# One more wait ahead of each scatter in the expert phase of an attention and mixture-of-experts kernel

## What is computed

```python
x = x + cross_attention(ctx_768, layernorm(x), mask)        # 64 batches of 128 tokens, width 256
h = layernorm(x)                                            # 8192 tokens
topk_idx, topk_w = route(h)                                 # 4 of 32 experts for each token
gate_vals = silu(h @ gate_w[e].T); up_vals = h @ up_w[e].T  # 128 wide
expert_out = (gate_vals * up_vals) @ down_w[e].T            # 256 wide
mixed = (expert_out of the 4 chosen * topk_w).sum(1)
x = x + mixed + shared_expert(h)
```

## Time and profile before

| | us |
|---|---|
| median of 3 runs | 1436.4 (1429.46 to 1436.93) |
| the profiled execution, own time | 1446.1 |
| its span, first to last instruction | 1444.1 |
| mean granted TensorE clock, share of 2.4 GHz | 0.984 |
| PE / ACT / DVE / POOL busy, share of the span | 93% / 72% / 67% / 42% |

### The profile page before, as it was taken

The page is one execution under the profiler, slowest core; times in us unless marked ns, Lnnn a source line. Parts: engine busy times, 40 slices in busy tenths (PEclk is TensorE's granted clock), DMA queues, the critical chain, the costliest instruction groups (busy, mean ns, idle before and its releaser), DMA issues.

```text
span 1444.1 us, 33057 instructions
## 1 busy us (share of the span) xinstructions
PE 1341.7 (93%) x8730; PEld 1042.9 (72%) x8730; DVE 963.0 (67%) x4500; ACT 1042.4 (72%) x2861; POOL 610.4 (42%) x662
## 2 busy tenths in 40 slices
PE   7999999999999999999798989988888889989997
PEld 4666666666666676666587878878788878878886
DVE  5578888888888888887863444444444444447888
ACT  5999999999999999998515555555555655553432
POOL 1004544544444554454553555555555555550000
PEclk8999999999999999999899999999999999999998
DMA  7145455445445544544865444444444444419886
GB/s 263 71 144 179 144 182 189 148 146 181 163 137 177 181 139 155 181 150 163 317 206 188 142 144 146 145 143 138 146 143 144 145 137 142 119 31 339 302 296 228
DMA packets 145780, 246.78 MB, mean 171 GB/s; under 512 B 22075, under 2 KB 108477, under 8 KB 144960
## 3 DMA queue, kind: packets, MB, share of 16 engines
q1 hardware_dynamic: 119488, 177.25, 37.9%
q0 software_dynamic: 26112, 67.42, 13.5%
HBM read 104.30 MB, written 120.09 MB: 155 GB/s over the span
## 4 chain that ended last, share of the span: by engine, by line
PE 51%; ACT 35%; issue 9%; DVE 3%; another core or an unknown queue 1%; DMA 0%; POOL 0%; ACTq 0%; SPq 0%; DVEq 0%; POOLq 0%
PE psT L1018 10%; PE psS L1028 9%; PE ps L1018 9%; ACT arena L1151 7%; PE ps L901 5%; ACT arena L1159 5%; PE ps L1009 5%; PE psS L912 4%; ACT arena L1167 3%; ACT arena L1119 3%; ACT arena L1123 2%; ACT arena L1074 2%; PE psT L901 2%; ACT arena L1111 2%; ACT arena L1103 2%
## 5 line engine op out<-in xcount | busy, mean ns | idle before, releaser
L686 POOL DMA_INDIRECT expert_out<-pay,dest x288 | 283.7, 985 | 259.6 <-DVE pay L1866 100.0
L546 POOL DMA_INDIRECT lists<-pay,slot x168 | 171.4, 1021 | 212.1 <-PE psT L812 39.4
L1028 PE MATMUL psS<-arena,history 128*128 x576 | 182.1, 398 | 52.0 <-DVE history L1859 31.0
L1866 DVE TENSOR_SCALAR pay<-psS,dest 128x256 f32<-128x256 f32 x288 | 138.5, 481 | 85.6 <-PE psS L1028 80.1
L1018 PEld LDWEIGHTS ps<-pad,hist_j 128*128 128x128 f32 x1152 | 150.2, 194 | 17.8 <-ACT pad L1310 6.7
L1018 PEld LDWEIGHTS psT<-pad 128*128 128x128 f32 x1152 | 150.3, 193 | 14.8 <-ACT pad L1310 5.1
L1018 PE MATMUL ps<-pad,hist_j 128*128 128x128 f32 x1152 | 155.5, 278 | 3.6 <-ACT pad L1310 3.3
L1018 PE MATMUL psT<-pad 128*128 128x128 f32 x1152 | 154.4, 277 | 2.9 <-ACT pad L1310 2.7
L1028 PEld LDWEIGHTS psS<-arena,history 128*128 128x128 f32 x576 | 87.2, 191 | 70.2 <-issue 69.2
L546 POOL DMA_INDIRECT lists<-arena,slot x88 | 90.0, 1023 | 95.9 <-PE psT L812 21.2
L742 PE MATMUL ps<-arena 128*128 128x512 f32 x256 | 127.3, 620 | 2.0 <-ACT arena L1111 1.8
(11 more groups left out here) (238 smaller groups left out, 3320.6 us busy)
## 6 DMA issues: line engine op xcount, KB each, us to landing
lists<-pad SPq DMA_DIRECT2D x72, 516.0 KB, 6.2
pay<-lists SPq DMA_DIRECT2D x288, 129.0 KB
arena<-expert_out SPq DMA_DIRECT2D x32, 1024.0 KB, 6.8
pay<-pay SPq DMA_DIRECT2D x42, 384.0 KB
x<-in_x SPq DMA_DIRECT2D x32, 256.0 KB
out<-arena SPq DMA_DIRECT2D x32, 256.0 KB, 5.7
arena<-arena SPq DMA_DIRECT2D x20, 384.0 KB
arena<-in_ctx SPq DMA_DIRECT2D x32, 192.0 KB
```

The lines of the kernel that those rows point to most:

```text
L546: pool.indirect_dma_start(lists, bass.IndirectOffsetOnAxis(ap=slots(u)[:, j, k:k + 1], axis=0), paid(u)[:, j, k, :], None).then_inc(scat[3 ...
L686: pool.indirect_dma_start(expert_out, bass.IndirectOffsetOnAxis(ap=dest[:, t % DESTS, 1:2], axis=0), yy[n], None, bounds_check=T * TOPK - ...
L1028: pe.matmul(dbank[n % 2][:, 0:D], hh[:, n % 4, :], w_dn[:, at(e, 1), :].rearrange("p a n -> p (a n)"), start=True, stop=True)\
L1866: dve.tensor_scalar(yy[n], dbank[n % 2][:, 0:D], dest[:, t % DESTS, 0:1].bitcast(fp32), None, ALU.mult)\
```

## The change

One wait is added ahead of each scatter of the expert phase. `gu_full` counts finished `gate_up` products, so `gu_full >= t + 3` means that the product of tile t + 2 is done; for the last tiles `upto` caps the value at 288. No instruction is moved, added or removed apart from the wait, on any engine.

```diff
             def scatter_tile(t, n):
                 pool.wait_ge(dest_kept, t + 1)
                 pool.wait_ge(yy_done, t + 1)
+                pool.wait_ge(gu_full, upto(t + 3, TILES))
                 pool.indirect_dma_start(
                     expert_out, bass.IndirectOffsetOnAxis(ap=dest[:, t % DESTS, 1:2], axis=0),
                     yy[n], None, bounds_check=T * TOPK - 1, oob_is_err=False).then_inc(y_out[n], 16)
```

## The result

The changed kernel takes 1418.3 us in the median of 5 runs (1416.26 to 1419.96), the kernel before 1435.2 us in 5 runs beside it (1429.46 to 1436.93). The ratio is 0.9883, 95% interval 0.9862 to 0.9904: **faster by 1.2%, 16.9 us**. The prediction was 1372 us, with 64 us of gain. The time lies in its range and the sign is right; the size is off: 16.9 us came of the 64 that were forecast, and the time is 46 us above 1372.

The account below looks back on a forecast made before the run. PE's 1.54 us a tile was the floor, with late PE semaphores behind close scatters making it 1.837. Gain 287 x 0.223 = 64 us, from the median 1436.4 - 64 = 1372 us; range 1350 to 1455.

Parts of the forecast that it names:

- Pace and floor: Expert phase: 1.837 us a tile, of which PE's own work is 1.54; recovering all the rest would give 85 us.
- PE's news comes late: A PE semaphore falling into a scatter begun while the one before is carried out is held until scatters nearly run dry.
- some 0.4 us or more into it: How far into such a closely following scatter a PE semaphore must fall to be held.
- The wait costs nothing: POOL's added condition: taken as nothing, at most 0.05 us a tile, 14 us.
- The step that failed: POOL can't run ahead of PE's products: two close scatters remain possible, but a third must wait for PE.
- Three tiles in four at 1.54: Expert phase: three tiles in four at 1.54 us, one at 1.837, so 1.614 us a tile and 64 us gained.
- not over 95: Sign of being right: PE's share of the expert phase rises above 95%, from 89%.
- not under 60: Sign of being right: ACT's idle time behind PE's products falls from 174 us to under 60.
- What would show it wrong: A product ending 0.7 us into a scatter being held when the scatter before began 1.54 us ahead of it.
- Rival 2: Bunches of scatters stay but holds shorten, saving 0.1 us a tile, 29 us: 1407 us (1395 to 1425); chance 0.26.
- Rival 3: No effect: a fixed price per scatter, or only a port is contended for; 1436 us within 0.5%; chance 0.11.
- rival 4: The wait locks scatter and product together, so products are held more often: 32 us slower, 1468 (1445 to 1490); chance 0.21.

Follow-up runs that it names:

- plain_store_d: Kernel before without POOL's 288 scatters; SP stores results by plain transfers to rows in tile order: 1361.6 us, against 1449.7 us for the kernel before.
- wait_next: Changed kernel, each scatter waiting for the gate-and-up product three tiles on, not two: 1359.6 us (before 1360.2), later 1422.0 us (before 1453.4).
- the spacing: Kernel before, POOL clearing a 320-column scratch buffer behind each scatter, no added wait: 1359.1 us (before 1360.2), later 1410.9 us (before 1453.4).
- the second 34: The changed kernel itself timed once more beside the kernel before: 1422.5 us against 1456.6 us, ratio 0.9782.
- gap_164_c: Kernel before, POOL clearing a 430-column scratch buffer behind each scatter, keeping scatters at least 1.64 us apart: 1389.5 us, against 1451.3 us before.
- wait_down: Changed kernel, each scatter waiting for the next tile's down product instead of the gate-and-up product two on: 1359.9, 1360.0, 1360.6 and 1361.7 us.

## Why the prediction was partly wrong

- **Pace and floor were right.** 1.837 us a tile, 1.54 of them PE's own, 85 us recoverable: plain_store_d gave 88 us and a phase with PE busy for 99.7%. In the series without holds wait_next stood at 1.54 us a tile, from 770.8 to 1212.8.
- **"PE's news comes late" behind close scatters was right, and incomplete.** plain_store_d shows that the scatters are the cause, the spacing that their distance matters. What the prediction couldn't see is the second condition: in four series of nine, nothing was held at 1.29 us either. And its "some 0.4 us or more into it" fits the second scatter of a bunch only. Less than 0.4 us into the second, 84 of 85 products of the changed kernel are free; 0.4 to 1.0 us into it, 38 of 43 of the kernel before are held. In the third scatter there is no such limit: all 26 products of the kernel before that end less than 0.2 us into it are held, by 1.6 to 3.1 us, and all 87 of the changed kernel that end less than 1.2 us into it. So the place in the bunch counts too.
- **The wait costs nothing: right.** Where nothing is held, wait_next stands at 0.9999 (0.9987 to 1.0012) of the kernel before. The changed kernel itself wasn't timed in such a series.
- **The step that failed** is the sentence "two scatters close together remain possible, when two products are let go together, but a third must wait for PE". It must, but PE's product is there. The scatter of 1003.28 is that of tile 133; it needs the product of tile 135, which ended at 1002.20, 1.50 us behind the bunch's first scatter and 1.08 us before POOL could begin the third. I had counted which scatters a held product stops, and not when the next, free one arrives. The third scatter then stands at the held product's place, and the bunch feeds itself as before.
- **From it follows the size.** "Three tiles in four at 1.54" was chosen, not derived. The steady stretches are as rare as before: 7 of the 287 distances between scatters are 1.50 to 1.58 us, where the kernel before has 10. PE's share of the phase is 93.8%, not over 95, and ACT's wait 176.5 us, not under 60. No row of before stood behind the three in four, so that the time still fell into the range 1350 to 1455 owes more to its width than to the sum.
- **What would show it wrong** was named: a product 0.7 us into a scatter 1.54 us behind the last. The trace of after has that row with both answers, in the timeline of PE and of ACT:

```profile
985.84 1.05 PE L1019 MATMUL ps<-pad,hist_j 128*128 128x128 f32 x8
987.38 1.05 PE L1019 MATMUL psT<-pad 128*128 128x128 f32 x8
```

```profile
986.93 0.28 ACT L1322 ACTIVATE history<-ps 128x128 f32<-128x128 f32 x1 [0.47 <-PE ps L1019]
...
989.16 0.28 ACT L1322 ACTIVATE history<-psT 128x128 f32<-128x128 f32 x1 [1.17 <-PE psT L1019]
```

  The first ends at 986.89, 0.68 us into the scatter of 986.21, and is free. The second ends at 988.43, 0.68 us into that of 987.75, and is held by 0.69 us. Of six such products in the trace, four are free and two held. The steady rhythm stands on the edge, so it lasts a few tiles and tips over.
- **Rival 2 came true.** It said that bunches stay and a hold shortens, 0.1 us a tile and 29 us. The traces show 0.107 and 30.7 us, the medians of the first comparison 17 and of the second 34. Its picture was half right: the bunches are of three, not pairs, with gaps of 2.6 us, and the hold ends 1.76 us behind the last scatter's start (1003.28 to 1005.04) where it had put 1.5 behind the second's.
- **Rival 3 falls, rival 4 too.** The time moved by 1.2% and 2.2%, clear of its interval. A fixed price per scatter is excluded by the spaced versions. The rule weighed in the prediction, from the Trainium skill (SBUF — State Buffer, SBUF: two separate sides), is about ports and may well hold: PE wasn't slowed here. But the run without scatters shows that ACT, which by it waits for nobody, sat idle behind what POOL had issued, and that this cost the kernel 88 us: what was late was PE's semaphore. Rival 4's lock never showed: waits on three different results of PE gained in every series with holds.

## What to carry to other kernels

When a consumer sits idle for one or two microseconds behind a producer that is plainly done, look at what another engine issued just then, and take that work out in one run before reasoning on its rhythm: here that one run gave the cause and the size of the whole prize, though its output isn't the kernel's. To break a bunch with a wait, write down for each of its members when the awaited event happens, the unhindered ones too; a wait that is met early holds nobody. And time the kernel before in several series, since a difference between series, here 5.5 to 7%, can be larger than what the change itself does.

## What the runs showed of the hardware

- **Two kinds of series.** Before took 1435.2, 1456.6, 1453.4, 1449.7 and 1451.3 us in five series, and 1360.2, 1360.1, 1359.8 and 1362.3 in four, with under 1% between the runs of one. One chip was in both groups (1453.4 and 1449.7 once each, 1360.1 between them), and the expert phase begins at the same time in both (first scatter at 768 to 776 us). The four without holds are just those that had wait_down beside them. Were it chance, that would come out in one of 126 ways to choose four series of nine; how another version could do it isn't known, and it wasn't tried alone. What decides stays open.
- **Where semaphores of PE were held.** Counted over the gate-and-up products of the phase, held being a silu over 0.12 us behind the product's end with ACT idle. Changed kernel: scatters 1.29 us apart, product ending 0.4 to 1.2 us into one, 82 held and 1 free. Kernel before: over 2.2 us behind the last scatter, 70 free and none held. Spaced at 1.53 us (series with holds), 0.2 to 1.4 us in: 135 held and 36 free, so more than the half that the expectation of gap_164_c has. wait_next in the series without holds, 1.29 us apart: 25 free, none held.
- **Records go missing along with it.** The traces hold about 25,000 changes of semaphores in the series without holds and 14,800 to 15,800 in the others, and 21,985 for the version without the expert phase's scatters in a series with holds. They are missing in the attention phase already: up to 764 us the traces of series with holds, plain_store_d among them, have 8,450 to 8,600, and the others 11,570 to 11,730, though that phase takes the same time in both kinds. In its expert phase plain_store_d has as many as the traces without holds (26 a us, where the changed kernel has 10). So the kind of series shows before the first scatter of the expert phase. Whether recording itself takes part in the holds can't be told from traces.
- **A scatter's own cost doesn't change.** 984 to 985 ns in the median where products are held, 982 to 983 where not (versions without spacing); at the closest 1.29 us from one to the next in both.
